# 16-feature attention: scores as two 64-row products in two PSUM banks, one buffer of scores

## The reference

```python
q = (query @ Wq).reshape(b, sq, 32, 16).transpose(0, 2, 1, 3)
k = (key @ Wk).reshape(b, sk, 8, 16).transpose(0, 2, 1, 3)      # and v alike
k = jnp.repeat(k, 4, axis=1)                                    # 4 query heads share a key head
scores = jnp.einsum('bhqd,bhkd->bhqk', q, k) * 16 ** -0.5
probs = jax.nn.softmax(scores, axis=-1)
out = jnp.einsum('bhqk,bhkd->bhqd', probs, v).transpose(0, 2, 1, 3).reshape(b, sq, 512)
x = x + jnp.tanh(g_xattn[layer]) * (out @ Wo)
```

## Time and profile before

| | us |
|---|---|
| median of 3 runs | 1869.24 |
| fastest and slowest run | 1868.93, 1880.10 |
| span of the profiled execution, its own time | 1874.3 |
| the 32 steps of the first attention, first scores to last update | 43.5 to 170.1 |
| the same of the second attention | 257.6 to 383.9 |
| granted TensorE clock over the span, as a share of 2.4 GHz | 0.943 |

### The profile page before, as it was taken

One profiled execution on the slowest core, in us unless ns is written; L12 is line 12 of the kernel. 1 busy time (PEld: TensorE's weight loads), 2 busy tenths in 40 slices (PEclk: granted clock), 3 DMA queues, 4 the chain that ended last, 5 costly groups with the idle time before them and its releaser, 6 DMA issues. The chain is left out here.

```text
span 1874.3 us, 27882 instructions
## 1 busy us (share of the span) xinstructions
PE 1667.6 (89%) x9746; PEld 1406.1 (75%) x9746; DVE 987.0 (53%) x1857; ACT 731.4 (39%) x2015; POOL 655.1 (35%) x594
## 2 busy tenths in 40 slices
PE   5998889856799989999999975699999999999986
PEld 4776667644598888888989863588888888888863
DVE  4885668778333313313323358665564654656553
ACT  3443254344353444525435434342433533424331
POOL 2542244465223212304212211353543543436320
PEclk9998999977799999999999995699999999999996
DMA  5001110010001000101000001000100011000001
GB/s 191 1 1 45 40 34 1 1 59 12 34 24 57 24 24 23 40 19 45 23 23 24 23 18 45 34 34 23 56 29 27 34 36 42 34 22 34 1 4 45
DMA packets 13132, 60.26 MB, mean 32 GB/s; under 512 B 1712, under 2 KB 2224, under 8 KB 8048
## 3 DMA queue, kind: packets, MB, share of 16 engines
q1 hardware_dynamic: 12176, 58.46, 9.0%
q10 hardware_dynamic: 864, 0.53, 0.1%
HBM read 56.89 MB, written 2.10 MB: 31 GB/s over the span
## 5 line engine op out<-in xcount | busy, mean ns | idle before, releaser
L373 PE MATMUL bank<-hid_high,wq_high 128*128 128x256 f32 x1152 | 343.2, 298 | 0.6 <-POOL wq_low L867 0.5
L373 PE MATMUL bank<-hid_low,wq_high 128*128 128x256 f32 x1152 | 326.5, 283 | 0.0
L373 PE MATMUL bank<-hid_high,wq_low 128*128 128x256 f32 x1152 | 326.4, 283 | 0.0
L1126 DVE SCALAR_TENSOR_TENSOR x_stream<-bank,gates,x_stream 128x512 f32<-128x512 f32 x128 | 96.1, 751 | 290.2 <-PE bank L373 290.2
L373 PE MATMUL bank<-wo_high,out_high 128*128 128x512 f32 x576 | 235.5, 409 | 15.0 <-DVE out_low L1118 11.8
L373 PEld LDWEIGHTS bank<-hid_high,wq_high 128*128 128x128 f32 x1152 | 221.4, 192 | 11.0 <-issue 10.4
L911 POOL TENSOR_TENSOR probs_middle<-probs_middle,small 128x512 f32<-128x512 f32 x64 | 66.6, 1040 | 463.9 <-DVE small L1113 463.9
L373 PE MATMUL bank<-wo_low,out_high 128*128 128x512 f32 x576 | 226.1, 393 | 0.0
L373 PE MATMUL bank<-wo_high,out_low 128*128 128x512 f32 x576 | 226.0, 392 | 0.0
L373 PEld LDWEIGHTS bank<-hid_low,wq_high 128*128 128x128 f32 x1152 | 221.6, 192 | 4.8 <-issue 4.6
L373 PEld LDWEIGHTS bank<-hid_high,wq_low 128*128 128x128 f32 x1152 | 221.1, 192 | 0.0
(11 more groups left out here) (236 smaller groups left out, 3551.4 us busy)
## 6 DMA issues: line engine op xcount, KB each, us to landing
raw_q<-in_L_wq SPq DMA_DIRECT2D x18, 1024.0 KB, 4.7
raw_o<-in_L_wo SPq DMA_DIRECT2D x18, 1024.0 KB, 4.8
raw_c<-in_L_wkv SPq DMA_DIRECT2D x14, 512.0 KB, 3.4
x_stream<-in_x SPq DMA_DIRECT2D x8, 256.0 KB, 10.1
out_x<-x_stream SPq DMA_DIRECT2D x8, 256.0 KB, 2.8
raw_q<-in_ctx_t SPq DMA_DIRECT2D x2, 512.0 KB, 4.7
raw_o<-in_ctx_t SPq DMA_DIRECT2D x2, 512.0 KB, 6.8
raw_c<-in_F_ar SPq DMA_DIRECT2D x2, 512.0 KB, 5.1
```

The lines of the kernel that those rows point to most:

```text
L373: last = k.nc.tensor.matmul(out, stationary(a, c), moving(b, c), start=n == 0, stop=n == total - 1)
L1126: nc.vector.scalar_tensor_tensor(xt, k.bank[7][:], gate, xt, ALU.mult, ALU.add).then_inc(k.x_done, 1)
```

## The change

The keys' mask gets 4 columns instead of 8: partition p belongs to block (p / 16) mod 4. `KBD` is then 4 blocks of 64 columns, in which partitions 0 to 63 hold key heads 0 to 3 and partitions 64 to 127 hold heads 4 to 7, in the same columns. `scores` becomes two products, one over partitions 0 to 63 into columns 0 to 255 of bank 0 and one over partitions 64 to 127 into the same columns of bank 1; the second signals. Both banks are taken by every step, so `scores(n)` now waits for the subtraction of step n-1. `maximum` reads the two half banks as one pattern of 2 x 4 x 64. In the built program the two products are placed at rows 0 and 64 of the array, as tiles of 64 rows by 128 columns; those of L713 before took 128 by 128.

```diff
--- before.py
+++ after.py
@@ -53,11 +53,13 @@
         self.o = [sb("out_high", 1024, F32R), sb("out_low", 1024, F32R)]
         self.ident, self.ones = sb("ident", P), sb("ones", P)
         self.causal = sb("causal", P)
-        self.kmask, self.vmask = sb("kmask", 8), sb("vmask", 512)
+        self.kmask, self.vmask = sb("kmask", 4), sb("vmask", 512)
         self.rope = sb("rope", 4 * S)
         self.gates = sb("gates", 8)
         self.small = sb("small", 256)
-        self.bank = [ctx.enter_context(nc.psum_tensor(f"bank{i}", [P, 512], F32)) for i in range(8)]
+        self.pair = ctx.enter_context(nc.psum_tensor("pair", [P, 1024], F32))
+        self.bank = [self.pair[:, 0:512], self.pair[:, 512:1024]]
+        self.bank += [ctx.enter_context(nc.psum_tensor(f"bank{i}", [P, 512], F32)) for i in range(2, 8)]
         def sem(name):
             self.base[name] = 0
             return ctx.enter_context(nc.semaphore(name))
@@ -443,7 +445,8 @@
 
     Q = k.q[:].rearrange("p (a g b r n) -> p a g b r n", a=2, g=2, b=4, r=2)
     KT = k.kt[:, 0:1024].rearrange("p (b n) -> p b n", b=B)
-    KBD = k.kt[:, 1024:2048].rearrange("p (a j n) -> p a j n", a=2, j=J)
+    KBD = k.kt[:, 1024:1536].rearrange("p (a j n) -> p a j n", a=2, j=J // 2)
+    SCORES = k.pair[:].rearrange("p (g j n) -> p g j n", g=2, j=J)[:, :, 0:J // 2, :]
     VTD = k.vt[:].rearrange("p (b e n) -> p b e n", b=B, e=2)
     VBD = k.vj[:, 0:1024].rearrange("p (a i n) -> p a i n", a=2, i=4)
     E = k.e[:].rearrange("p (a j n) -> p a j n", a=5, j=J)
@@ -483,8 +486,8 @@
             def keys(b):
                 if b >= 2:
                     pool.wait_ge(k.s_psum, k.at("s_psum", 2 * (b - 1)))
-                nc.gpsimd.tensor_tensor(KBD[:, b % 2], KT[:, b:b + 1, :].broadcast_to([P, J, S]),
-                                        k.kmask[:].rearrange("p (j a) -> p j a", a=1).broadcast_to([P, J, S]),
+                nc.gpsimd.tensor_tensor(KBD[:, b % 2], KT[:, b:b + 1, :].broadcast_to([P, J // 2, S]),
+                                        k.kmask[:].rearrange("p (j a) -> p j a", a=1).broadcast_to([P, J // 2, S]),
                                         ALU.mult).then_inc(k.kbd_ready, 1)
 
             keys(0)
@@ -630,12 +633,12 @@
                 dve.wait_ge(k.s_psum, k.at("s_psum", n + 1))
                 if n >= RING:
                     dve.wait_ge(k.pt_psum, k.at("pt_psum", n - RING + 1))
-                sp_ = k.bank[n % 2][:].rearrange("p (j n) -> p j n", j=J)
                 mx = sc[:, 128 + 8 * (n % 2):136 + 8 * (n % 2)]
-                nc.vector.tensor_reduce(mx, sp_, AX, ALU.max).then_inc(k.vec_step, 1)
+                nc.vector.tensor_reduce(mx.rearrange("p (g j) -> p g j", g=2), SCORES, AX, ALU.max).then_inc(k.vec_step, 1)
                 k.base["vec_step"] += 1
                 dve.wait_ge(k.vec_step, k.base["vec_step"])
-                nc.vector.tensor_tensor(E[:, n % RING], sp_, mx.rearrange("p (j a) -> p j a", a=1).broadcast_to([P, J, S]),
+                nc.vector.tensor_tensor(E[:, n % RING].rearrange("p (g j) n -> p g j n", g=2), SCORES,
+                                        mx.rearrange("p (g j a) -> p g j a", g=2, a=1).broadcast_to([P, 2, J // 2, S]),
                                         ALU.subtract).then_inc(k.max_ready, 1)
 
             def total(n):
@@ -708,10 +711,13 @@
                 b, rp, p = n // 2, n % 2, n // 8
                 pe.wait_ge(k.kbd_ready, k.at("kbd_ready", b + 1))
                 pe.wait_ge(k.q_sbuf, k.at("q_sbuf", 2 * p + 2))
-                if n >= 2:
-                    pe.wait_ge(k.max_ready, k.at("max_ready", n - 1))
-                nc.tensor.matmul(k.bank[n % 2][:], Q[:, p % 2, rp, b % 4, :, :],
-                                 KBD[:, b % 2], start=True, stop=True).then_inc(k.s_psum, 1)
+                if n >= 1:
+                    pe.wait_ge(k.max_ready, k.at("max_ready", n))
+                for g in range(2):
+                    rows = slice(64 * g, 64 * g + 64)
+                    last = nc.tensor.matmul(k.bank[g][:, 0:256], Q[rows, p % 2, rp, b % 4, :, :],
+                                            KBD[rows, b % 2], start=True, stop=True)
+                last.then_inc(k.s_psum, 1)
 
             def transposes(n):
                 pe.wait_ge(k.p_ready, k.at("p_ready", n + 1))
@@ -2216,7 +2222,7 @@
 
     same = (ar(P)[:, None] // S) == (ar(P)[None, :] // S)
     causal = np.where(same & (ar(P)[None, :] <= ar(P)[:, None]), 0.0, NEG).astype(np.float32)
-    kmask = (ar(P)[:, None] // 16 == ar(8)[None, :]).astype(np.float32)
+    kmask = (ar(P)[:, None] // 16 % 4 == ar(4)[None, :]).astype(np.float32)
     pair = 2 * ar(4)[None, :, None] + (ar(P) // S)[:, None, None]
     vmask = (pair == (ar(P) // 16)[None, None, :]).astype(np.float32).reshape(P, D)
     inv = (np.float32(1.0) / np.float32(10000.0) ** (ar(0, P, 2, dtype=np.float32) / np.float32(P))).astype(np.float32)
```

## The result

The changed kernel takes 1883.59 us (median of 8 runs, 1879.64 to 1886.32), the one before 1874.37 in runs beside it: a ratio of 1.005 (1.0033 to 1.0067), about 9 us slower. That is no change by the bound of 1%, but the interval leaves no doubt that it is a loss. The profiled execution spans 1879.7 us against 1874.3.

The account below looks back on a forecast made before the run. PE was taken to set the pace, DVE 2.6 us behind in four steps. Start +2.0 and steady part +1.4 gave +3.4 us a stage, +6.8 for two: 1869.24 + 6.8 = 1876 us, range 1861 to 1890.

Parts of the forecast that it names:

- the class: Whole kernel: no change by the bound of 1%, 18.7 us; chance 0.83.
- The product itself: Scores on PE: the two products take 0.64 us instead of 0.86, a gain of 0.22 us a step.
- Only A2 and B1 can overlap: Scores run as A1, A2, B1, B2, two MATMULs per product; only the middle two run together: 3 x 0.214 = 0.64 us.
- the rival to which 0.15 was given: Scores: both products run wholly side by side, slot 0.43 us, -1 us a stage, 1867 us; chance 0.15.
- The switch: PE's array changing shape around scores, twice a step: about 0.15 us each, +0.30 us a step, from 0 to 0.56.
- The steady part: Attention steps 6 to 28: +0.25 us in four steps, +1.4 us a stage.
- The single buffer, steady part: Scores waiting for the previous step's subtraction between the ends of a stage: PE does not wait, so no cost.
- other work: PE's work between two scores, 3.0 us even in its shortest interval, said to cover the wait for DVE.
- the chain of 2.37 us: From the start of scores through DVE's reduction and subtraction back to PE: 2.37 us, so PE does not wait.
- The single buffer, start: Start of each attention stage, where PE lacks filler: scores 2 comes 2.3 us late; +2.0 us a stage, ends 1.0 and 2.4.
- The tail: Last steps, from about 26 on: filler is missing, but PE sits behind the last probabilities anyway; cost 0.
- The smaller parts: POOL's masked keys fall from 1043 ns to between 520 and 1043; DVE's PSUM reads cost the same; DMAs untouched.

Follow-up runs that it names:

- The buffer alone: Kernel before the change, with only the wait changed: scores(n) waits for the subtraction of step n-1, not n-2; 1885.6 us, ratio 1.0072.
- the 128-row products: Changed kernel with both scores products over all 128 rows, the mask at 8 columns again, no change of shape or overlap; 1883.56 us.

## Why the prediction was right, and where it was not

1876 us was forecast and 1883.6 measured, 1874.4 beside it: +6.8 against +9.2. Of the 7.6 us between the two times, 5.1 are the base, which was 1869.24 in three runs and 1874.37 in eight. The sign, the class and the range held. Of the steps behind them several failed, and in both directions.

**The product itself: failed.** "Only A2 and B1 can overlap" does not hold. The slot is 0.64 us, the very number forecast for the product alone, but by luck: it is 0.43 of whole overlap and 0.21 of switches, where 0.79 was to be seen for 0.64 and a switch. MATMULs start in pairs, 7 ns apart, one of either tile; the overlap saves 0.41 us, not 0.22. This was the rival to which 0.15 was given. Its time, 1867, is wrong too, for what follows.

**The switch: right, a little low.** 0.15 us was taken from one weight load in another stage; it is 0.34 for the two of a step, 0.17 each on average. Eight switches cost 1.36 us in four steps and eat most of the 1.64 that the overlap gives.

**The steady part: sign wrong.** +0.25 in four steps was forecast; measured is -0.17: 1.36 - 1.64 = -0.28, of which the growing wait for `values` gives back 0.1 (the 0.16 of L738 in the timeline above). From n = 6 to 26 that is -0.87, not +1.2.

**The single buffer, steady part: right.** No wait between the ends, 14.80 to 14.83 in the kernel with the wait alone. (The 3.0 us of "other work" run from start to start and have the slot of scores in them; so has the chain of 2.37, and the comparison holds.)

**The single buffer, start: half of it.** Scores 2 was forecast 2.3 us late, measured 2.43. But the stage is 4.6 late at n = 6, since the clock falls in these waits: the 24 query products take 48.88 to 54.17 at half clock. I had put this into the range with 1.6 us and left it out of the sum. **This is the term that was wrong:** the start was taken at +2.0 us and measured +4.6 and +4.5, about 2.1 of it behind scores 2, in both stages. The buffer alone and the 128-row products show the cause, the idle MATMULs the share of the clock.

**The tail: 0, but not for the reason given.** From n = 26 to the last update the stages lose -0.2 and +0.4 us. But at n = 28 they had lost 1.5 and 1.6 more. Scores 27 waits 1.8 us for the buffer, yet that wait is not the loss: the second stage of the timed kernel with idle MATMULs has the wait and no loss at n = 28, at a clock of 1.00 (its second row above), and so has the kernel with the buffer alone; the first stage of the kernel with a second pair in the tail has no wait and loses 1.62. The loss goes with a fall of the clock between scores 27 and 28. It is there in 13 of the 18 stages in the traces of kernels with two row tiles side by side, and in none of the 8 in those without tiles of 64 rows. Behind n = 31 it comes back, for the clock moved: before had it at 0.50 there, after has its fall earlier. Windows 132:142 and 142:158 read 1.00 and 0.89 in before, 0.88 and 0.97 in after.

**The smaller parts: right.** The masked keys take 0.61 us, and DVE's two-bank reads cost nothing that shows: its reduction takes 0.68, as before.

**The account.** Start +4.6, steady -0.9, tail -0.2 and +0.4: +3.6 and +4.0, against +3.4 forecast. It came near by luck, because errors of opposite sign met: 2.6 us too little at the start, 2.3 too much in the steady part. The two stages grew by 7.6 us and the profiled span by 5.4; 0.5 came between them, 0.9 were won ahead of the first and 1.8 behind the second. How the 9.2 us between the medians divide, one trace of each can't tell.

## What to carry to other kernels

Row tiles did run wholly side by side here, but on a PE that works in several shapes each change of shape cost some 0.17 us (float32, 2.4 GHz), so what a pair of products saves must exceed two of them; here 0.41 us of overlap stood against 0.34 of switches. Where a change puts PE into a wait, or merely shortens its work, ahead of a run of products, price those products at half the clock as well: scores 2 was 2.4 us late, and 2.1 more came behind it at the low clock. When a variant wins time in stages that it doesn't touch, look there before you praise it: here the waits put down to "issue" told that gain from the change's own.

## What the runs showed of the hardware

- Float32 products of two row tiles, written one behind the other, ran in pairs of MATMULs 7 ns apart, and so did their weight loads. The Trainium skill, TensorE: Matmul & The Clock Gate, Part 3, gives some 4 ns for each further tile; here it is 7.
- Idle MATMULs in two waits kept PE at 2.4 GHz in three of four starts (0.57 over 262 to 266 us in the fourth), and the start lost 1.3 to 2.6 us instead of 4.5.
- Scores on two row tiles with unchanged waits came with a clock of 0.86 over 12 us instead of 1.00; PE was busy for 8.90 us instead of 9.83.
- A stop of 2.23 us within a run of eight MATMULs, with the low clock behind it, is worth 3.3 to 4.0 us, and comes and goes with edits in other stages. That it is the loading of code is likely, not shown.
